# Layer 0 of a two-layer kernel: two DRAM places for the halves, low halves behind the sums, and ScalarE rounding both 8-bit grids

## What is computed

```python
x = x + tanh(g_xattn[0]) * L0_xattn(layernorm(x), ctx, causal, padding, ...)   # 32 heads of 8, 8 key groups
x = x + tanh(g_ffn[0])   * L0_ffn(layernorm(x), w_up, w_down)

def act_quant(x, bits):                      # per token, 8 bits
    scale = 127 / clip(max(abs(x)), EPS, None)
    return clip(round(x * scale), -127, 127) / scale

def hbitlinear(x, w, bits):                  # w to -1, 0, 1 times its mean size
    return act_quant(fwht(x), bits) @ weight_quant(w).T
h = relu(hbitlinear(hidden, w_up, 8)) ** 2   # 256 -> 512
return hbitlinear(h, w_down, 8)              # 512 -> 256
```

## Time and profile before

| | us |
|---|---|
| median of 3 runs | 1274.64 |
| lowest, highest | 1269.18, 1277.73 |
| the profiled execution | 1274.92 |
| its span, first to last instruction | 1272.9 |
| busy in the span: TensorE, weight loads, VectorE, ScalarE, GpSimd | 1126.0, 909.1, 1059.2, 918.8, 736.3 |
| mean granted TensorE clock, of full speed | 0.967 |

### The profile page before, as it was taken

How to read it: one execution, slowest core, us unless ns; L and a number is a source line. 1 busy time by engine, 2 the same in 40 slices (tenths; PEclk the granted TensorE clock), 3 DMA queues, 4 the chain that set the end, 5 groups by cost and what they waited for, 6 DMA issues and landing times. The chain is left out here.

```text
span 1272.9 us, 30350 instructions
## 1 busy us (share of the span) xinstructions
PE 1126.0 (88%) x8831; PEld 909.1 (71%) x8831; DVE 1059.2 (83%) x2469; ACT 918.8 (72%) x3601; POOL 736.3 (58%) x1084
## 2 busy tenths in 40 slices
PE   2688888877899999999999999999899999659992
PEld 2345555544588888888888888888787788549981
DVE  6689999988798898998898888899689888766664
ACT  3556666658899889989989989987788888213330
POOL 5357777776756665665665665665445787323331
PEclk9889999999999999999999999999899999879996
DMA  6445554442230312220330220220311100633326
GB/s 165 88 81 78 84 77 79 76 69 49 72 105 1 88 32 57 87 66 21 87 87 0 87 87 0 87 87 31 110 52 59 35 35 31 254 95 82 96 68 202
DMA packets 135320, 97.04 MB, mean 76 GB/s; under 512 B 59070, under 2 KB 128832, under 8 KB 135233
## 3 DMA queue, kind: packets, MB, share of 16 engines
q1 hardware_dynamic: 125680, 84.18, 26.6%
q0 software_dynamic: 3408, 8.45, 1.8%
q10 hardware_dynamic: 6144, 3.35, 0.9%
HBM read 55.02 MB, written 41.56 MB: 76 GB/s over the span
## 5 line engine op out<-in xcount | busy, mean ns | idle before, releaser
L1543 POOL TENSOR_TENSOR head_rstd<-head_rstd,minus_half 128x4 f32<-128x4 f32 x192 | 224.8, 1171 | 15.0
L1531 ACT ACTIVATE squares<-ps 128x128 bf16<-128x128 f32 x768 | 202.5, 285 | 42.7 <-PE ps L1494 35.5
L1494 PE MATMUL ps<-w_proj_in,xq 128*128 128x512 f16 (+1 forms) x1024 | 209.9, 328 | 6.0 <-ACT headsT L1567 5.4
L1623 POOL TENSOR_TENSOR prob<-prob,rinv 128x512 f32<-128x512 f32 x128 | 140.5, 1098 | 109.0 <-DVE rinv L1618 108.8
L1610 ACT ACTIVATE prob<-ps,nmax 128x128 f32<-128x128 f32 x512 | 182.6, 391 | 9.6 <-DVE nmax L1601 8.2
L1567 ACT ACTIVATE headsT<-ps,l_hln 128x256 f32<-128x256 f32 (+1 forms) x256 | 168.2, 691 | 29.2 <-PE ps L1558 29.2
L1531 ACT ACTIVATION_READ_ACCUMULATOR squares<-ps 128x1 f32 x768 | 165.5, 216 | 0.0
L1551 DVE TENSOR_TENSOR heads_n<-ps,head_rstd 128x512 f32<-128x512 f32 x192 | 131.3, 684 | 25.0 <-POOL head_rstd L1543 24.8
L1494 PEld LDWEIGHTS ps<-w_proj_in,xq 128*128 (+1 forms) x1024 | 100.0, 98 | 53.3 <-issue 9.1
L1594 PE MATMUL ps<-headsT 128*128 128x128 f32 x1024 | 137.0, 277 | 1.1 <-DVE probT L1639 0.4
L1594 PEld LDWEIGHTS ps<-headsT 128*128 128x128 f32 x1024 | 128.9, 193 | 8.1 <-issue 5.5
(11 more groups left out here) (320 smaller groups left out, 2597.1 us busy)
## 6 DMA issues: line engine op xcount, KB each, us to landing
slots<-blank_slot SPq DMA_DIRECT2D x12, 1554.0 KB, 8.5
halves<-half_made SPq DMA_DIRECT2D x32, 256.0 KB, 2.5
w_proj_in<-halves SPq DMA_DIRECT2D x16, 512.0 KB, 9.0
w_out_raw<-in_wprojT SPq DMA_DIRECT2D x8, 512.0 KB, 3.9
half_raw<-in_winT SPq DMA_DIRECT2D x16, 256.0 KB, 3.0
half_raw<-in_woutT SPq DMA_DIRECT2D x16, 256.0 KB, 3.1
taken<-slots SPq DMA_DIRECT2D x15, 259.0 KB, 3.4
q_rows<-q_parts SPq DMA_DIRECT2D x48, 64.0 KB
```

The lines of the kernel that those rows point to most:

```text
L1494: last = e.matmul(out, xq[:, k, which, slot_at], weights(k, hl, c0, n), start=(k == 0 and hl == 0), stop=(k == KD - 1 and hl == 1))
L1531: last = e.activation(squares[:, 4 * n + h, :], A[n][:, h * HD1:(h + 1) * HD1], ACT.Square, scale=HD1**-0.5, accum_out=hss[:, 4 * n + h:4 ...
L1543: e.tensor_tensor(hr[:, four], hr[:, four], t["half"][:, four], ALU.pow).then_inc(g_r[n].sem, 1)
L1623: e.tensor_tensor(prob[:, kind, :, :], prob[:, kind, :, :], spread(rinv[:, kind, :], P), ALU.mult).then_inc(g_p[kind].sem, 1)
```

## The change

OUT, INS and INT use place `p` of two in DRAM; OUT stores the k halves twice, so that the two halves of `k_rows` are loaded by one DMA. OUT's wait for the loads of the item before goes; INS and INT wait for their own loads of the item before instead. `k_rows` is laid out group first. The two wide operations of each grid are now ScalarE pieces, F3r and F6r; the four small steps stay on VectorE. On GpSimd WL goes behind F3b. On SP LW goes behind CT. On TensorE F4 goes behind ST:2 and F4u behind S:3. `MIXED` has the new pieces put in for ScalarE.

```diff
 ORDER0 = {
     "tensor": (
...
-        "S:1+ ST:1 S:2+ F4-- ST:2 OB:1- F4u-- S:3+ ST:3 S:4+ OT- ST:4 S:5+ F7--- W- S:6+ S:7+ F7d--- PV:0 "
+        "S:1+ ST:1 S:2+ ST:2 F4-- OB:1- S:3+ F4u-- ST:3 S:4+ OT- ST:4 S:5+ F7--- W- S:6+ S:7+ F7d--- PV:0 "
...
-        "EX:5 P2a+++ F2a- EX:6 EX:7 P3h+++ OC:1 EX:0+ EX:1+ F4a- EX:2+ F4s- OTa WH++ F7a-- EX:3+ NTh++ EX:4+ "
+        "EX:5 P2a+++ F2a- EX:6 F6r-- EX:7 P3h+++ OC:1 EX:0+ F3r- EX:1+ EX:2+ F4a- F4s- OTa WH++ F7a-- EX:3+ NTh++ EX:4+ "
...
-    "gpsimd": "XB+ F5v-- F1g- WL+ F3b- VC++ PD+ P1g++++ WC++ F7s-- F4v-",
-    "sync": "INS- ROW-- INT- LW OUT CT++",
+    "gpsimd": "XB+ F5v-- F1g- F3b- WL+ VC++ PD+ P1g++++ WC++ F7s-- F4v-",
+    "sync": "INS- ROW-- INT- OUT CT++ LW",
...
-    kT = sb("k_rows", [P, 2, 2, G0, P], F16)
+    kT = sb("k_rows", [P, 2, G0, 2, P], F16)
...
-    q_parts = nc.dram_tensor("q_parts", [2, D, P], F16, kind="Internal").ap()
-    k_parts = nc.dram_tensor("k_parts", [2, G0 * HD0, P], F16, kind="Internal").ap()
+    q_parts = nc.dram_tensor("q_parts", [2, 2, D, P], F16, kind="Internal").ap()
+    k_parts = nc.dram_tensor("k_parts", [2, 2, G0 * HD0, 2, P], F16, kind="Internal").ap()
...
     @s.piece("OUT", "sync")
     def _(e, i, p):
         e.wait_ge(v_part.sem, v_part.at(i))
-        e.wait_ge(d_ins.sem, d_ins.at(i - 1))
-        e.wait_ge(d_int.sem, d_int.at(i - 1))
         for part in range(2):
-            e.dma_start(q_parts[part].rearrange("(m p) t -> p m t", p=P), q_part[:, part, :, :]).then_inc(d_out.sem, 16)
-        e.dma_start(k_parts.rearrange("n f t -> f n t"), k_part[:, :, :]).then_inc(d_out.sem, 16)
+            e.dma_start(q_parts[p, part].rearrange("(m p) t -> p m t", p=P), q_part[:, part, :, :]).then_inc(d_out.sem, 16)
+        for hf in range(2):
+            e.dma_start(k_parts[p, :, :, hf, :].rearrange("n f t -> f n t"), k_part[:, :, :]).then_inc(d_out.sem, 16)
...
     @s.piece("INS", "sync")
     def _(e, i, p):
         e.wait_ge(d_out.sem, d_out.at(i))
         e.wait_ge(pe_S.sem, pe_S.at(i - 2))
+        e.wait_ge(d_ins.sem, d_ins.at(i - 1))
...
         e.wait_ge(pe_ST.sem, pe_ST.at(i - 2))
+        e.wait_ge(d_int.sem, d_int.at(i - 1))
         for n, (q, k) in enumerate(parts):
-            for hf in range(2):
-                e.dma_start(kT[n * HD0:(n + 1) * HD0, p, hf, :, :], of_group(k)).then_inc(d_int.sem, 16)
-            e.dma_start(qT[n * HD0:(n + 1) * HD0, p, :, :], q_parts[q].rearrange("(h d) t -> d h t", d=HD0)).then_inc(d_int.sem, 16)
+            e.dma_start(kT[n * HD0:(n + 1) * HD0, p, :, :, :].rearrange("d g h t -> d g (h t)"), of_group(p, k)).then_inc(d_int.sem, 16)
+            e.dma_start(qT[n * HD0:(n + 1) * HD0, p, :, :], q_parts[p, q].rearrange("(h d) t -> d h t", d=HD0)).then_inc(d_int.sem, 16)
...
     @s.piece("F3", "tensor")
     def _(e, i, p):
         e.wait_ge(g_sum.sem, g_sum.at(i))
-        e.wait_ge(v_q2.sem, v_q2.at(i - 1))
+        e.wait_ge(a_g2.sem, a_g2.at(i - 1))
...
-    def quantise(e, chain, quant, src, norm, c, rnd, out, done):
+    def step_of(e, chain, quant, src, norm, c):
         chain.link(e.tensor_reduce(quant[:, c:c + 1], src, AX, ALU.max, apply_absolute_value=True))
         chain.link(e.tensor_scalar(quant[:, c:c + 1], quant[:, c:c + 1], norm, EPS, ALU.mult, ALU.max))
         chain.link(e.reciprocal(quant[:, c + 1:c + 2], quant[:, c:c + 1]))
-        chain.link(e.tensor_scalar(quant[:, c + 2:c + 3], quant[:, c + 1:c + 2], norm, 127.0, ALU.mult, ALU.mult))
-        chain.link(e.tensor_scalar(rnd, src, quant[:, c + 2:c + 3], MAGIC, ALU.mult, ALU.add))
-        e.tensor_scalar(out, rnd, MAGIC, None, ALU.subtract).then_inc(done.sem, 1)
+        chain.last(e.tensor_scalar(quant[:, c + 2:c + 3], quant[:, c + 1:c + 2], norm, 127.0, ALU.mult, ALU.mult))
...
+    @s.piece("F3r", "scalar")
+    def _(e, i, p):
+        e.wait_ge(c_f3.sem, c_f3.at(i))
+        e.activation(rnd1[:, :], F1[:, 0:D], ACT.Copy, bias=MAGIC, scale=quant[:, p, 2:3]).then_inc(a_g1.sem, 1)
+        e.wait_ge(a_g1.sem, a_g1.at(i, 1))
         e.wait_ge(pe_q1.sem, pe_q1.at(i - 1))
+        e.activation(q1[:, :], rnd1[:, :], ACT.Copy, bias=-MAGIC).then_inc(a_g1.sem, 1)
...
+    @s.piece("F6r", "scalar")
+    def _(e, i, p):
+        e.wait_ge(c_f6.sem, c_f6.at(i))
+        e.activation(rnd2[:, :], F1[:, :], ACT.Copy, bias=MAGIC, scale=quant[:, p, 6:7]).then_inc(a_g2.sem, 1)
+        e.wait_ge(a_g2.sem, a_g2.at(i, 1))
         e.wait_ge(pe_q2.sem, pe_q2.at(i - 1))
+        e.activation(q2[:, :], rnd2[:, :], ACT.Copy, bias=-MAGIC).then_inc(a_g2.sem, 1)
```

More of the change, by code:

```diff
@@ L65, in link, with last, at @@
         self.engine.wait_ge(self.sem, self.i * self.per + self.n)
+    def last(self, instruction):
+        instruction.then_inc(self.sem, 1)
+        self.n += 1
+    def at(self, i):
+        return i * self.per + self.per
     def end(self):
@@ L437, in _ @@
         for hf in range(2):
-            last = e.activation(kT[LOW:P, 0, hf, :, :], tiled(low8[LOW:P, hf, :], G0), ACT.Copy, scale=UP)
+            last = e.activation(kT[LOW:P, 0, :, hf, :], tiled(low8[LOW:P, hf, :], G0), ACT.Copy, scale=UP)
         last.then_inc(laid, 1)
@@ L487, in _ @@
         for hf in range(2):
-            last = e.tensor_scalar(kT[LOW:P, 1, hf, :, :], tiled(low8[LOW:P, hf, :], G0), UP, 0.0, ALU.mult, ALU.add)
+            last = e.tensor_scalar(kT[LOW:P, 1, :, hf, :], tiled(low8[LOW:P, hf, :], G0), UP, 0.0, ALU.mult, ALU.add)
         last.then_inc(blocks, 1)
@@ L547, in _ @@
         e.tensor_scalar(bq[:, :], bq[:, :], HD0**-0.5, None, ALU.mult).then_inc(ready, 1)
-        e.memset(kT[TOP:LOW, :, :, :, :].rearrange("p s h g t -> p (s h g t)").bitcast(F32), UP_PAIR).then_inc(ready, 1)
+        e.memset(kT[TOP:LOW, :, :, :, :].rearrange("p s g h t -> p (s g h t)").bitcast(F32), UP_PAIR).then_inc(ready, 1)
         e.wait_ge(w_mask, W_MASK)
@@ L887, in _ @@
             some = slice(hf * HF, (hf + 1) * HF)
-            last = e.matmul(bank[:, :, some], kT[:, p, hf, g, :], qT[:, p, g * R0:(g + 1) * R0, some], start=True, stop=True)
+            last = e.matmul(bank[:, :, some], kT[:, p, g, hf, :], qT[:, p, g * R0:(g + 1) * R0, some], start=True, stop=True)
         last.then_inc(pe_ST.sem, 1)
@@ L1029, in _ @@
         e.wait_ge(pe_h1.sem, pe_h1.at(i))
+        step_of(e, c_f3, quant[:, p, :], F1[:, 0:D], D**-0.5, 0)
+        c_f3.end()
+    @s.piece("F3r", "scalar")
[3 more added lines that the diff above has]
+        e.wait_ge(a_g1.sem, a_g1.at(i, 1))
         e.wait_ge(pe_q1.sem, pe_q1.at(i - 1))
-        quantise(e, c_f3, quant[:, p, :], F1[:, 0:D], D**-0.5, 0, rnd1[:, :], q1[:, :], v_q1)
-        c_f3.end()
+        e.activation(q1[:, :], rnd1[:, :], ACT.Copy, bias=-MAGIC).then_inc(a_g1.sem, 1)
     @s.piece("F4v", "gpsimd")
     def _(e, i, p):
-        e.wait_ge(v_q1.sem, v_q1.at(i))
+        e.wait_ge(c_f3.sem, c_f3.at(i))
         e.tensor_tensor(quant[:, p, 3:4], quant[:, p, 0:1], w_step[:, 0:1], ALU.mult).then_inc(g_two.sem, 1)
@@ L1042, in _ @@
     def _(e, i, p):
-        e.wait_ge(v_q1.sem, v_q1.at(i))
+        e.wait_ge(a_g1.sem, a_g1.at(i))
         e.wait_ge(a_yT.sem, a_yT.at(i))
@@ L1058, in _ @@
         e.wait_ge(a_q1.sem, a_q1.at(i))
-        e.wait_ge(v_q1.sem, v_q1.at(i))
-        filling(e, i, (v_q2, -1), (v_x2, -2), (a_q2, -2))
+        e.wait_ge(a_g1.sem, a_g1.at(i))
+        filling(e, i, (a_g2, -1), (v_x2, -2), (a_q2, -2))
         for m in range(KF):
@@ L1098, in _ @@
         e.wait_ge(g_two.sem, g_two.at(i))
+        step_of(e, c_f6, quant[:, p, :], F1[:, :], quant[:, p, 7:8], 4)
+        c_f6.end()
+    @s.piece("F6r", "scalar")
[3 more added lines that the diff above has]
+        e.wait_ge(a_g2.sem, a_g2.at(i, 1))
         e.wait_ge(pe_q2.sem, pe_q2.at(i - 1))
-        quantise(e, c_f6, quant[:, p, :], F1[:, :], quant[:, p, 7:8], 4, rnd2[:, :], q2[:, :], v_q2)
-        c_f6.end()
+        e.activation(q2[:, :], rnd2[:, :], ACT.Copy, bias=-MAGIC).then_inc(a_g2.sem, 1)
     @s.piece("F7", "tensor")
     def _(e, i, p):
-        e.wait_ge(v_q2.sem, v_q2.at(i))
+        e.wait_ge(a_g2.sem, a_g2.at(i))
         if not isinstance(i, int) or i + 1 < B:
             e.wait_ge(a_hid.sem, a_hid.at(i + 1))
-        filling(e, i, (v_q1, 1), (v_q2, 0), (v_x2, -1))
+        filling(e, i, (a_g1, 1), (a_g2, 0), (v_x2, -1))
         for k in range(KF):
```

34 lines of the change are left out of this document (14 added, 20 removed).

## The result

The kernel after takes 1289.14 us in the median of four runs (1284.87 to 1290.32), the one before 1273.12 beside it; the ratio is 1.0119, 95% interval 1.0102 to 1.0136. It is slower by a little over 1%; I had forecast 1269 and a range up to 1280, and had given a loss of over 1% a chance of 0.06.

The account below looks back on a forecast made before the run. It took VectorE, nearly full, and GpSimd's row as both tight in the even turns, ScalarE fullest in shared ones. Even turns -4.7, start +1, shared turns -2 sum to -5.7 us: 1269, range 1254 to 1280.

Parts of the forecast that it names:

- The even turns: Layer 0's steady turns, walked step by step from F6: 16.45 us each, 0.42 less; eleven turns save 4.7 us.
- The ring of LW, 16.46: In an even turn, the loop from P3v's end through OUT, LW's landing, WM, F2 and grids takes 16.46 us, setting the turn.
- The start. I take +1 us: Before the steady turns: LW ahead of INS and ROW against an earlier OUT, +1 us, bounds -2 and +3.
- LW's first issue at 10.7, not 7.22: On SP in a turn, LW behind OUT and CT issues its first load 10.7 us after F6 instead of 7.22.
- The shared turns: I take -2: Turns layer 0 shares with layer 1, 265 to 348 us: -2 us, bounds -6 and +6.
- the `yfly` wait: In the shared turns, TensorE's wait for F3b behind WL; F3b ahead of WL gives back up to 4 us.
- the bound of +6: Slower limit for the shared turns, where ScalarE, 15.73 of 17 busy, gets 2.2 us more in each of five turns.
- ScalarE becomes the bound (slower): At F3r on ScalarE: +5 us in even turns, +4.5 shared, +1 start, giving 1285 us; chance 0.13.
- WL holds VectorE in its new place: F3q's small steps wait for WL; with WL 1.5 later, 0.6 us a turn, about 1275, no change; chance 0.15.
- GpSimd's ring rules (faster): ScalarE reaches F3r without waiting and GpSimd's row sets the even turn at 15.4 us, giving 1256; chance 0.22.
- The two places in DRAM: OUT goes once P3v is done; the replacement waits of INS and INT, for loads a turn old, cost nothing.
- OUT(1) goes 2.2 earlier: At the start, OUT of item 1 goes 2.2 us earlier, weighed against LW's 2.8 us of issues.

Follow-up runs that it names:

- f3_early: `both` with F3r ahead of OC:1 on ScalarE, F4a right behind EX:0, F4 and F4u two score products sooner on TensorE; 1258.74 us, ratio 0.9908 to the kernel before.
- lw_old: The changed kernel with LW back in its old place on SP, between INT and OUT; 1280.99 us, ratio 1.0052 to the kernel before.
- tail_load: `both` with spare ScalarE copies of about the grids' length, which nobody waits for, in F3r's and F6r's places in the shared turns; ratio 0.9991 to the kernel before.
- both: The changed kernel with LW in its old place on SP and the grids' wide operations back on VectorE in the shared turns; ratio 0.9939 to the kernel before.
- wl_only: The kernel before with one edit, WL behind F3b on GpSimd; ratio 1.0053 to the kernel before.
- wl_dram: `wl_only` plus the changed kernel's OUT, INS and INT with two DRAM places; ratio 1.0005 to the kernel before.
- tail_vec: The changed kernel with the grids' wide operations back on VectorE in the shared turns only; ratio 1.0009 to the kernel before.

## Why the prediction was wrong

- **The even turns: right.** Each step of the walk came within 0.15 us, and with it the reason for the small gain: the 1.3 us won by F6q are given back because F3r stands behind OC:1 and EX:0. `f3_early` shows it from the other side: with that order changed the turn is 0.6 to 0.7 us shorter.
- **The ring of LW, 16.46: the number met, the cause not.** F6 was ended by F7v on VectorE (line 1152, [0.22]), no wait for LW shows in an even turn, and `lw_old`, with LW early, has the same 16.39. In the turn shown above the last load of LW was issued at 210.95, and WM began at 213.86 without a wait. The loads landed sooner than the 3.4 us that I had taken (after, 95 to 265 us, from issue to landing: least, median, most):

```profile
DMA to landing us min/median/max: 1.9/2.1/2.5
```

- **"The start. I take +1 us": mis-sized, +4.8.** I weighed 2.8 us of issues against an earlier OUT. In the first turns LW is not only later by its neighbours' issues: it stands behind a wait of 5 us for the low halves, 3.2 in the even turn (202.14 to 205.35), and behind 3.16 us of `wo` loads, which an even turn doesn't have, and WM ahead of F2 waited 11.1 us in three. The step "LW's first issue at 10.7, not 7.22" had been taken from a steady turn.
- **"The shared turns: I take -2": this step failed, +13.0.** I counted ScalarE's 2.2 us more per turn against the `yfly` wait as two amounts of work. Both terms were wrong. Of the 4 us for `yfly` next to nothing came: what F3b had waited for last was ScalarE's copy of `ynT`, not WL. With WL moved and the grids on VectorE the wait fell from 9.5 to 8.6 and the stretch is 101.8 to 103.0, against 102.6; in after the wait grew to 11.8. And the bound of +6 had only work in it, for which `tail_load` shows 4.3. Left out was the place in line: ScalarE there serves two layers by a written order, and each grid now crosses between engines twice, VectorE to ScalarE and on to TensorE, where it crossed once, on the one chain through bank F1. That an engine 15.7 of 17 busy has no spare moment at the right time is how I explain it; what the runs show is the price, 5.5 us for F3's grid and 10.7 for F6's.
- **The rival "ScalarE becomes the bound (slower)": right place in part.** It put 4.5 us on the shared turns, all of it as load, and 5 on the even turns, where nothing of the sort happened. F3r cost 0.92 us there (0.50 + 0.42), not 1.6.
- **The rival "WL holds VectorE in its new place": right in mechanism, wrong on the operation.** It named F3q's small steps. In after they began at 203.22, just as WL had ended (203.11), and took 0.15 each. What WL holds is the wide operation of F6q from SBUF to SBUF, which the change had moved to ScalarE. With the rule of the Trainium skill that I cited, page "SBUF — State Buffer", section "SBUF: two separate sides", these rows agree: 2.18 us beside WL, and 0.43 and 0.51 in two shared turns of `both`, without it.
- **The rival "GpSimd's ring rules (faster)": what kept it away was the order, as it said against itself.** With F3r ahead of OC:1 the turn is 15.78, where the rival had 15.4.
- **The two places in DRAM: costed at nothing in a turn, rightly; at the start they are worth 3.5 us in the version `both`,** and 0.3 between `wl_only` and `wl_dram`. I had this only as "OUT(1) goes 2.2 earlier".

Open: why the medians lie 6 us further apart than the profiled executions; and how much of the 13 us belongs to TensorE's lower clock. For the same 617 matmuls TensorE was busy 83.5 us before (clock 0.97) and 89.7 after (0.88), so as an estimate (the ends are modelled) the clock can hold up to 6.2 of the 13 us, and up to 3.4 of the 4.3 in `tail_load` (0.95). It fell where TensorE stood waiting (0.57 from 340 to 350 of after, where TensorE was busy for 4.9 us of 10), and over the stretch it was 0.97 again in `tail_vec`. So I read it as a follower of the waits, but no run sets it apart.

## What to carry to other kernels

Walk a pipelined change through each stage whose order differs, not only through the steady one: the start has its own waits in the queue, and a stretch shared by two layers has its own full engine. Work moved to an engine that is nearly full costs more than its length when others wait for it: here two to four times the price of nearly the same load that nobody waits for. Before a wait is put down to a long operation, look whether the engine stood idle behind that operation: GpSimd did, for `ynT`, so having WL out of its way gave next to nothing. And moving a long GpSimd operation away from one VectorE operation only helps if what it meets next isn't of the same kind; look at every wide one from SBUF to SBUF in the new place.

## What the runs showed of the hardware

Not every operation of VectorE is held by a long one of GpSimd. In after, beside WL (200.98 to 203.11), VectorE's statistics of 256 columns (line 705, begun at 200.80, before WL) took 0.43 and the row maxima out of PSUM (from 201.91) 0.69, as elsewhere; in `wl_only` the 512 columns from SBUF to SBUF, 32 to 16 bits, took 2.18. In these runs it is decided by which of the two begins first. In `both` the same operation of VectorE took 2.36 us when it began 0.04 us behind GpSimd's (260.51); when it began 0.18 us ahead, it took 0.49, and GpSimd's took 2.31 instead of 2.12:

```profile
298.04 0.49 DVE L1129 TENSOR_SCALAR q<-rnd 128x512 bf16<-128x512 f32 x1
```

```profile
298.22 2.31 POOL L1211 TENSOR_TENSOR w_proj_in<-unit_raw,w_proj_in 128x1024 f16<-128x1024 f32 x1
```

The same loads of LW that land in 2.2 us (median, after, 24 to 96 us) behind OUT and CT took 4.2 in `lw_old`, right behind INT, over the same stretch: here the landing time changed with the place in the queue. On ScalarE the rounding with a scale per row took 0.69 for 512 columns and 0.47 for 256, where the plain operations of these sizes took 0.60 and 0.38; the second of each pair 0.63 and 0.42.
